# One program for projection and attention, with attention's first operands loaded during the last projection heads

## The reference

```
B, T, C = x.shape                 # 1, 2048, 512
H, HKV, HD = (16, 4, 128)
G = H // HKV                      # 4 query heads for each key head
q = (x @ Wq + bq).reshape(B, T, H, HD)
k = (x @ Wk + bk).reshape(B, T, HKV, HD)
v = (x @ Wv + bv).reshape(B, T, HKV, HD)
q = _rope(q, cos, sin)
k = _rope(k, cos, sin)
scores = jnp.einsum('bgjtd,bjsd->bgjts', q, k) * scale
scores = jnp.where(mask[None, None, None], scores, -jnp.inf)
wei = jax.nn.softmax(scores, axis=-1)
out = jnp.einsum('bgjts,bjsd->bgjtd', wei, v)
...
return out @ Wo + bo
...
x = _layernorm(x + attention(x))
x = _layernorm(x + experts(x))    # 64 experts, top 8, capacity 256
```

## Time and profile before

| | us |
|---|---|
| median of three runs | 2221.84 |
| lowest and highest run | 2221.49 and 2221.94 |
| the profiled execution | 2223.41 |
| its span, first to last instruction | 2221.5 |
| TensorE busy | 2042.8 (92%) |
| VectorE busy | 1623.7 (73%) |
| ScalarE busy | 1363.1 (61%) |

### The profile page before, as it was taken

One profiled execution on the slowest core, in us unless ns is written; L12 is line 12 of the kernel. 1 busy time (PEld: TensorE's weight loads), 2 busy tenths in 40 slices (PEclk: granted clock), 3 DMA queues, 4 the chain that ended last, 5 costly groups with the idle time before them and its releaser, 6 DMA issues. The chain is left out here.

```text
span 2221.5 us, 40794 instructions
## 1 busy us (share of the span) xinstructions
PE 2042.8 (92%) x13314; PEld 1816.8 (82%) x13314; DVE 1623.7 (73%) x3105; ACT 1363.1 (61%) x2735; POOL 875.8 (39%) x821
## 2 busy tenths in 40 slices
PE   8999969999999999999999998998938999999990
PEld 6888858898889988889888988777727999999980
DVE  5899967877678767787677775545545888888874
ACT  3677756766667656666567664322315777777771
POOL 1000013333233322333233332266664777777760
PEclk9999979999999999999999999999968999999995
DMA  7555563110520105201251000875616999999987
GB/s 247 193 214 212 211 233 123 53 62 20 181 100 25 63 22 196 84 25 58 79 194 67 30 20 25 315 260 189 218 60 200 296 291 302 296 291 303 295 218 244
DMA packets 142151, 361.84 MB, mean 163 GB/s; under 512 B 17809, under 2 KB 35217, under 8 KB 137361
## 3 DMA queue, kind: packets, MB, share of 16 engines
q1 hardware_dynamic: 109200, 292.27, 37.6%
q0 software_dynamic: 32768, 67.26, 12.6%
HBM read 223.55 MB, written 136.05 MB: 162 GB/s over the span
## 5 line engine op out<-in xcount | busy, mean ns | idle before, releaser
L630 PE MATMUL p_S<-p_kT,p_q 128*128 128x512 f32 (+3 forms) x1920 | 475.5, 378 | 26.0 <-DMA p_q<-qk_scratch 19.7
L630 PEld LDWEIGHTS p_S<-p_kT,p_q 128*128 128x128 f32 x1920 | 325.1, 191 | 75.6 <-issue 21.6
L822 POOL TENSOR_SCALAR p_prob<-p_prob,p_inv 128x128 f32<-128x128 f32 (+7 forms) x256 | 192.7, 753 | 468.6 <-DVE p_inv L770 468.6
L822 POOL TENSOR_SCALAR p_prob<-p_prob,p_inv,p_part 128x1024 f32<-128x1024 f32 x128 | 153.7, 1201 | 494.4 <-DVE p_inv L775 494.4
L642 PE MATMUL p_TP<-p_ident,p_prob 128*128 128x128 f32 x2176 | 303.6, 274 | 1.8 <-DVE p_pT1l L781 1.8
L1525 POOL DMA_INDIRECT sum_scratch<-p_y,p_tokT x128 | 235.6, 1840 | 84.5 <-ACT p_y L1392 64.6
L759 DVE TENSOR_REDUCE p_nmax<-p_S 128x1 f32<-128x1024 f32 (+7 forms) x256 | 251.9, 984 | 22.8 <-PE p_S L630 21.8
L642 PEld LDWEIGHTS p_TP<-p_ident,p_prob 128*128 128x128 f32 x2176 | 245.6, 141 | 26.0 <-DVE p_pT1l L781 5.6
L717 ACT CAST p_pT1h<-p_TP 128x512 fp32r<-128x512 f32 (+3 forms) x320 | 154.9, 526 | 152.8 <-PE p_TP L642 152.6
L717 ACT CAST p_pT0h<-p_TP 128x512 fp32r<-128x512 f32 (+3 forms) x320 | 155.3, 527 | 150.1 <-PE p_TP L642 148.9
L661 PE MATMUL p_O<-p_pT0h,p_v 128*128 128x256 f32 x1088 | 227.5, 293 | 6.0 <-DVE p_pT0l L781 6.0
(11 more groups left out here) (214 smaller groups left out, 4536.7 us busy)
## 6 DMA issues: line engine op xcount, KB each, us to landing
p_w_raw<-in_gu SPq DMA_DIRECT2D x64, 768.0 KB
qk_scratch<-p_qout SPq DMA_DIRECT2D x80, 512.0 KB, 2.6
o_scratch<-p_oT SPq DMA_DIRECT2D x128, 256.0 KB, 2.1
p_ot<-o_scratch SPq DMA_DIRECT2D x32, 1024.0 KB
p_q<-qk_scratch SPq DMA_DIRECT2D x15, 2048.0 KB, 9.3
p_w_raw<-in_gu SPq DMA_DIRECT2D x64, 256.0 KB
v_scratch<-p_vout SPq DMA_DIRECT2D x16, 512.0 KB, 3.2
p_t_raw<-in_dn SPq DMA_DIRECT2D x32, 256.0 KB
```

The lines of the kernel that those rows point to most:

```text
L630: mm = nc.tensor.matmul(out, x, y, start=(n == 0), stop=(n == 2))
L822: nc.gpsimd.tensor_scalar(prob[k][:, cols], prob[k][:, cols], inv[:, k:k + 1], scale, ALU.mult, ALU.mult).then_inc(normed, 1)
```

## The change

Projection and attention become two parts of one program, as routing and experts already are: a new function `attention` makes the tiles and semaphores of both and runs, on each engine, first the projection's list and then attention's. Tiles get fixed addresses. kT, v's first part and q0 lie where the value projection's tiles lay (3 to 51 KB of each partition), q1 where qout lay (167 KB and up). Identity, mask and their bf16 copies are made once, in the projection.

The four key heads are projected first, so that head n of the loop is key head n for n < 4 and query head n - 4 behind that; the constant arrays are put in this order. The query heads of key head 0 are loop heads 4 to 7. From head 8 to head 12 SP issues one load for attention behind each head's weight load: keys 0, q0 (2 MB), values 0, keys 1, values 1. The first of them waits for all value stores and for the stores of heads 0 to 7. q1 waits for all stores (`stored`).

For the first key head, PE's scores now wait for `k_in0` and q_in[0], weighing for `v_in0`, and take_k and take_v are left out. The two casts to identb and maskb stand on ACT ahead of head 0 of the projection.

```diff
+EARLY = 8
...
+            sp.dma_start(maskf[:], mask_d).then_inc(own.mask_in, 16)
             with sp.Fori(2, NB // 2) as i:
...
+            def head_step(i, between=(), last=False):
                 for k in range(2):
                     n = i * 2 + k
                     if not last:
                         sp.wait_ge(w_lo, n + 1)
                         sp.dma_start(w_raw[k][:], wqk[bass.ds(n + 2, 1)].rearrange("o p m -> (o p) m")
                                      ).then_inc(w_in[k], 16)
+                    if k < len(between):
+                        between[k](sp)
                     for t in range(NT):
...
-            with sp.Fori(0, NH // 2 - 1) as i:
-                head_step(i, False)
-            head_step(NH // 2 - 1, False, last=True)
+            with sp.Fori(0, EARLY // 2) as i:
+                head_step(i)
+
+            def keys(sp):
+                for k in range(2):
+                    sp.wait_ge(v_out[k], 16 * (NB // 2))
+                    sp.wait_ge(q_out[k], 16 * NT * (EARLY // 2))
+                preload[0](sp)
+
+            head_step(EARLY // 2, (keys, preload[1]))
+            head_step(EARLY // 2 + 1, (preload[2], preload[3]))
+            head_step(EARLY // 2 + 2, (preload[4],))
+            with sp.Fori(EARLY // 2 + 3, NH // 2 - 1) as i:
+                head_step(i)
+            head_step(NH // 2 - 1, last=True)
+
+        def stored(sp):
+
             for k in range(2):
-                sp.wait_ge(v_out[k], 16 * (NB // 2))
                 sp.wait_ge(q_out[k], 16 * NT * (NH // 2))
...
+            act.wait_ge(ident_in, 16)
+            nc.scalar.copy(identb[:], ident[:]).then_inc(own.mask_ready, 1)
+            act.wait_ge(own.mask_in, 16)
+            nc.scalar.copy(maskb[:], maskf[:]).then_inc(own.mask_ready, 1)
...
+        def first_k(sp):
+            sp.dma_start(kT[:, 0].bitcast(F32), qk_d[0, :, 0]).then_inc(k_in0, 16)
+
+        def first_v(sp):
+            sp.dma_start(v[:, 0:4].bitcast(F32), v_d[0:4, 0].rearrange("b p h d -> p b h d")).then_inc(v_in0, 16)
+
+        preload = (first_k, lambda sp: load_q(sp, 0, 0), first_v, lambda sp: load_k(sp, 0, 1),
+                   lambda sp: load_v(sp, 0, 1))
...
             def head(j, first=False, last=False):
-                if not first:
+                if first:
+                    stored(sp)
+                    load_q(sp, j, 1)
+                else:
                     sp.wait_ge(scored, j * SG[U])
...
-                if u == 0:
-                    pe.wait_ge(k_first, j + 1)
+                if u == 0 and first:
+                    pe.wait_ge(k_in0, 16)
+                elif u == 0:
+                    pe.wait_ge(k_first, j)
...
-                if i == 0:
+                if i == 0 and not first:
                     take_k(j)
-                if i == (0 if first else WEIGH - 1):
-                    take_v(j, first)
+                if i == WEIGH - 1 and not first:
+                    take_v(j)
...
+        @block.sync
+        def _(sp):
+            project.sync(sp, preload)
+            attend.sync(sp, stored)
+
+        @block.tensor
+        def _(pe):
+            project.tensor(pe)
+            attend.tensor(pe)
```

More of the change, by code:

```diff
@@ L106, in sem @@
         def sem(name):
[L107 to L110 removed]
+            return sems.enter_context(nc.semaphore("p1_" + name))
+        ident, maskf, identb, maskb = own.ident, own.maskf, own.identb, own.maskb
+        bias = [sb(f"bias{k}", [P, 1], kb=2 + k / 32) for k in range(2)]
+        bias_v = [sb(f"bias_v{k}", [P, 1], kb=2 + (2 + k) / 32) for k in range(2)]
+        xraw = [sb(f"xraw{k}", [P, C], kb=3 + 2 * k) for k in range(2)]
         xt = [[sb(f"xt{k}{s}", [P, NC, P], F32R) for s in "hl"] for k in range(2)]
[L112 removed]
         wv_raw = sb("wv_raw", [P, NC * C])
@@ L127, in stage_project @@
         qr = [sb(f"qr{k}", [P, 512]) for k in range(NT)]
-        qout = [sb(f"qout{k}", [P, NT, 2, 512], F32R) for k in range(2)]
+        assert sb.end <= 167 * 1024
+        qout = [sb(f"qout{k}", [P, NT, 2, 512], F32R, kb=167 + 16 * k) for k in range(2)]
         pt = [ps(f"pt{k}", [P, NC, P]) for k in range(2)]
@@ L253, in _, with scalar @@
             loop(pe, NH // 2, head_step)
[L255 to L256 removed]
+        def scalar(act):
             for s in range(2):
@@ L484, in sem @@
         def sem(name):
[L485 to L491, removed]
+            return sems.enter_context(nc.semaphore("p2_" + name))
+        ident, identb, maskb = own.ident, own.identb, own.maskb
+        kT = sb("kT", [P, NT, 2, 512], F32R, kb=3)
         v = sb("v", [P, NB, 2, HD], F32R)
+        q = [sb(f"q{k}", [P, G, 2, 512], F32R, kb=(35, 167)[k]) for k in range(2)]
+        prob = [sb(f"prob{k}", [P, T], kb=51 + 8 * k) for k in range(KEEP)]
+        pT = [[sb(f"pT{k}{s}", [P, NB, 2, P], F32R) for s in "hl"] for k in range(2)]
+        oT = [sb(f"oT{k}", [P, 2, 2, P], F32R) for k in range(2)]
         k_next = sb("k_next", [P, 2, 512], F32R)
         v_next = sb("v_next", [P, 4, 2, HD], F32R)
[L495 to L498, removed]
+        assert sb.end == 167 * 1024
+        sb.end = 2 * 1024 + 256
         nmax, nmax1 = sb("nmax", [P, KEEP]), sb("nmax1", [P, KEEP])
@@ L504, in stage_attend @@
         inv = sb("inv", [P, KEEP])
+        assert sb.end <= 3 * 1024
         S = ps("S", [P, 2, 1024])
@@ L588, in head @@
                     if p == 5 and not last:
-                        sp.wait_ge(k_first, j + 1)
-                        sp.wait_ge(v_first, j + 1)
+                        if not first:
+                            sp.wait_ge(k_first, j)
+                            sp.wait_ge(v_first, j)
                         load_next(sp, j + 1)
@@ L643, in turn, with weigh @@
                 mm.then_inc(turned, 1)
-            def weigh(j, back, p, part, half=None):
+            def weigh(j, back, p, part, first, half=None):
                 nb = blk(2 * p) + 1
@@ L651, in weigh @@
                 if part == 0 and half != 1:
-                    if p == 0:
-                        pe.wait_ge(v_first, j + 1)
+                    if p == 0 and first:
+                        pe.wait_ge(v_in0, 16)
+                    elif p == 0:
+                        pe.wait_ge(v_first, j)
                     elif p % 8 == 0:
@@ L825, in _, with attention @@
             loop(pool, HKV, step)
+    return Programs(sync, tensor, scalar, vector, gpsimd), preload
+@dataclass
+class Own:
+    ident: object
+    maskf: object
+    identb: object
+    maskb: object
+    ident_in: object
+    mask_in: object
+    mask_ready: object
+def attention(nc, passed, x, wqk, wv, bv, cos, sin, ident_d, mask_d, qk_d, v_d, o_d, wo, wo_raw, wo_in, base):
+    with ExitStack() as sems:
+        sb = Place(nc, "p12_", base)
+        tiles = [sb("ident", [P, P]), sb("maskf", [P, P]), sb("identb", [P, P], BF16), sb("maskb", [P, P], BF16)]
+        own = Own(*tiles, *[sems.enter_context(nc.semaphore("p12_" + n)) for n in ("ident_in", "mask_in", "mask_ready")])
+        project, stored = stage_project(nc, base, own, sems, passed, x, wqk, wv, bv, cos, sin, ident_d, mask_d, qk_d, v_d)
+        attend, preload = stage_attend(nc, base, own, sems, passed, qk_d, v_d, o_d, wo, wo_raw, wo_in)
+        block = sems.enter_context(nc.Block())
+        @block.sync
[6 more added lines that the diff above has]
+            attend.tensor(pe)
+        @block.scalar
+        def _(act):
+            project.scalar(act)
+            attend.scalar(act)
+        @block.vector
+        def _(dve):
+            project.vector(dve)
+            attend.vector(dve)
+        @block.gpsimd
+        def _(pool):
+            project.gpsimd(pool)
+            attend.gpsimd(pool)
 def stage_route(nc, base, ident, sems, passed, x, wo, bo, rw, ident_d, lower_d, o_d, x1_d, sum_d, slot_d, wo_raw, wo_in):
```

104 lines of the change are left out of this document (40 added, 64 removed).

## The result

The changed kernel took 2207.35 us (median of four runs, 2206.82 to 2211.1), the kernel before, beside it on the same chip, 2221.89 (2221.49 to 2225.84). The ratio is 0.9939, with an interval of 0.9927 to 0.995: 14.5 us less. The forecast was 15.4 less. That is close, but the trace will show two terms in it that were not in the working, of opposite sign. The profiled execution took 2206.82 us, its span was 2204.9.

A forecast was written before the change was run, and what follows sets the result against it. PE was taken to bound the kernel, with a 19 us hole between projection and attention; 15.4 us counted at DVE's tail, other prices and clock 0, takes the median 2221.84 to 2206.4 us, range 2203.5 to 2211.

The forecast's parts named there:

- Removed from the path, 14.6 us at the first maximum: Attention's start: store wait, program change, loads and copies go; DVE's first row maximum moves from 304.07 to 289.45.
- 15.2 and 15.4 us at rows 2 and 3: Attention's first scores on PE: row 2 moves to 290.28, row 3 to 291.36; 15.4 us is carried on.
- The five loads, price 0: SP in projection heads 8 to 12: 4.2 MB of added loads fit in queue and engines, weight loads keep 1.9 us cover.
- 3 us if the weights are late and nobody recovers: Projection behind the q load: upper bound if weights land late and DVE recovers nothing; 0 was taken, recovery by head 19.
- The casts, the mask load, the start inside a loop, price 0: Casts (at most 0.6 us) and mask load hide before head 0; running into new code costs 0, at most 1 us.
- q1 with 8 us of cover: Second q tile, loaded after all stores, lands at 301.7; row 16 needs it at 311.1, cover 8 us or more.
- The clock, 0.50 in about 289 to 297, no difference: Attention's start: lower clock for about 9 us again, sum unchanged; bounds 3.0 us saved or about 1 us lost.
- projection ending at 284.0 as now: End of projection on PE: a sign that the last matmul stays at 284.0; later than 284.5 makes the prediction wrong.
- the clock did not stay up: Rival at attention's start: clock stays up through PE's 4 us pause, gain 15.4 + up to 3.0, 2203.4 to 2205.5; 8%.
- PE did stop: Rival at attention's start: PE never stops, first steps fill the hole, all 19.0 us gained, 2202.8; 2%.
- The queue was not late: Rival: crowded queue makes weights late in heads 11 and 12, or code starts late; costs 1 to 5 us, 2208 to 2212; 14%.
- The rival of the slower side: Preloads hold back weight loads of heads 11 to 15, four times 4 us reach PE, 2223 to 2230; 2%.

The follow-up runs named there:

- head 9 with all loads: Changed kernel with q0, values 0, keys 1 and values 1 (3.7 MB) all issued in head 9: 2188.43 us, projection 229.54.
- the busy PE: Changed kernel with twenty unread 512-column matmuls added on PE in the first key head at step 2: 2189.32 us, ratio 0.9958.
- The six kernels on addresses: Kernel before with new addresses or xT moved; changed kernel shifted 1,024 bytes, or weights 128, 64, or 128 alone: projection 229.53, 225.27, 229.54, 225.28, 228.63, 225.27.
- the two changed kernels of the first batch: Changed kernel with xT and all behind it 1,024 bytes higher, 2211.72 us; changed kernel with the five early loads issued after all stores, 2223.4 us.
- The repeat there: Changed kernel again, unedited, on the other chip: 2187.33 us in five runs against 2200.18 for the kernel before, ratio 0.9944.

## Why the prediction was right, and where its sum was off

The mechanism is the predicted one, and its size too. What the prediction called 15.4 us, the hole closed behind DVE's tail, was 15.6: the scores of row 4 moved by -11.16, and the projection's later end is +4.48 in it. The kernel without the early loads says the same from the other side: 14.2 of these 15.6 us go when the loads are late again. Step by step:

- *Removed from the path, 14.6 us at the first maximum:* -10.31 measured, -14.8 without those 4.48. DVE's gap to its last projection instruction is nothing, where 0.1 was allowed.
- *15.2 and 15.4 us at rows 2 and 3:* row 2 is scored at 294.59, and 290.28 + 4.48 is 294.76; row 3 at 295.39 for 295.84. Row 3 took 0.80 us behind row 2, not 1.03. All of q0 is there, as expected, and no idle time at the start is put down to a load.
- *The five loads, price 0:* right. SP's first one waited about 2 us for head 7's stores. With q0 in the queue the small weight load took 5.0 us to land in place of some 3, inside its cover; ACT waits for no load. Head 12 is the head where it was looked for:

```profile
p_w_raw<-in_wqk SPq DMA_DIRECT2D x1, 256.5 KB, 5.0
```

- *3 us if the weights are late and nobody recovers:* the recovery was an argument, and head 9 with all loads showed it: 2.8 us lost on DVE, none at head 19.
- *The casts, the mask load, the start inside a loop, price 0:* the first matmul of a head is 0.22 us later. More can't be said: among the kernels with one program, which have the same code ahead of that matmul, it comes anywhere from 64.31 to 66.94, so a price under 1 us would not be seen.
- *q1 with 8 us of cover:* issued at 297.18, landed in 8.9 us, the first maximum of row 16 at 315.45: 9.4 us of cover. That held at the pace of the changed kernel only; what it would have done to the stores behind it at a faster pace was not thought of, and the busy PE showed it.
- *The clock, 0.50 in about 289 to 297, no difference:* the place is right with the 4 us added (292.5 to 299.3). The low stretch with work in it is shorter than before's, and from row 4 to routing's start the changed kernel gains 0.4 us more: inside the bounds.

What failed is one sentence of the prediction's last part, "projection ending at 284.0 as now", and behind it the assumption that the projection's work keeps its pace. The row that it gave as its own test, a last matmul later than 284.5, says so: 288.46. The prediction costed what each engine does and waits for, and gave the fixed addresses no cost. They cost 4.3 us: the head weights lie at 157,376 bytes in each partition, 192 over a multiple of 256, in place of 154,432, 64 over one, and each of 960 matmuls takes 4.4 ns more. The six kernels on addresses show that it is this, and that 128 bytes take it away. The region of xT and the addresses of ACT's and DVE's tiles are ruled out; the period of the remainder is not settled. Why PE fetches or loads one stationary operand slower than the other is not settled. No kernel was made to vary xT's remainder.

With this term and the later first head the sum is 15.4 - 4.3 - 0.2 = 10.9, and 11.16 were measured at row 4, 11.59 at attention's end. The rest, 5.0 us in the profiled pair and 14.5 - 11.6 = 2.9 in the medians, came from where nothing was changed: routing took 271.93 us before and 267.52 after, the experts 520.70 and 520.15. It is the kernel before that stands apart here. With other addresses it took 268.57 and 267.74 us for routing, with the same order of the same work, and the two changed kernels of the first batch 267.20 and 267.04: of the six profiles with a routing of this length before's alone is over 269. Part of it goes with the clock at the start of routing (means 0.91, 0.96, 0.81 in three parts of it before, 0.96, 0.95, 0.81 after), but not all: the old code with new addresses has a mean of 0.91 in the first part too, and 268.57. Nor is it scatter between executions alone. The kernel without the early loads enters routing 3.4 us after the kernel before by the profiles, and is only 0.8 us slower by ten runs against 13. So some 3 us seem to be a property of the kernel before as it is laid out, which every edit here lost; that is argued, since no run took routing by itself, and why is open. On the other chip the kernel before was not profiled. The repeat there gives 12.85 us, with an interval (9.2 to 15.4 by its ratio) that holds both 11.6 and 15.4. So the number on record was hit partly by luck: a routing that was slow in the kernel before covered a term that was missing.

The rivals: the clock did not stay up, and PE did stop, for 5.4 us; with PE kept busy the clock was worth 1.3 to 1.7 us, half of the 3.0 that the bound gave. The queue was not late in the changed kernel. The rival of the slower side was tried in a hard form, and even 4 us of lateness in one weight load did not reach PE. No rival had the projection become slower.

## What to carry to other kernels

When a change moves tiles to other addresses, that is an edit with a price of its own: compare the spacing of the same matmuls in both traces, and if it differs, move the stationary operand by 128 bytes, which gave all of it back here (64 gave less than a quarter), before looking further. A hole between two stages closes only as far as the slowest engine's tail, so count the gain at the engine that feeds the next stage's first decision (here the row maximum on DVE) and not at PE. Read a fused or moved stage from its own boundaries, since the whole time can hide 4 us by a difference of the other sign elsewhere. And when a stage is made faster, look at what its small stores stand behind in the queue: a large load that was harmless at the old pace stops ACT at the new one.

## What the runs showed that was not expected

- The spacing of float32r matmuls of 512 columns depends on the byte address of the stationary operand: 228.9 ns at 64 over a multiple of 256, 233.3 ns at 192, and projection 228.63 us, between the two (225.28 and 229.54), at 0. A shift by 1,024 bytes, and one of ACT's and DVE's tiles by 128, change nothing.
- The end of one program and the start of the next cost little beside the loads and waits that stand there: SP's first load goes out 3.78 us behind DVE's last instruction with them and 3.37 without.
- A small store behind a 2 MB load on one queue cost ACT 2.46 us and PE 2.32.
- Routing with its many small transfers takes 267 to 272 us on one chip and 245 to 246 on another, in every kernel, while projection (at one address) and attention agree within 0.4% on both.
